# First sweep's rows 0 and 1 in 64-column halves, part of four norms on GpSimd, and constants and last stores on other queues

## The reference, cut to what matters

```python
# layer 0
u = par_u[0] * par_u[1] * (diag_u[:, None] * x[:2048] @ W_u) + x[:2048]     # the same for the other rows
e = concatenate([u, i])
h = adj @ (adj.T @ e)
x1 = layernorm(x + layernorm(h) * gamma + beta + x)
# layer 1, Chebyshev
T1 = adj @ x1
T2 = 2 * (adj @ T1) - x1
T3 = 2 * (adj @ T2) - T1
out = layernorm(x1 + x1 @ w[0] + T1 @ w[1] + T2 @ w[2] + T3 @ w[3] + bias)
```

## Time and profile before

| | us |
|---|---|
| median of 3 runs | 1199.03 |
| lowest and highest | 1196.73 and 1199.1 |
| profiled execution, its own time | 1196.89 |
| span of the profiled execution | 1195.1 |
| PE busy | 1105.3 (92%) |
| DVE busy | 920.1 (77%) |
| ACT, POOL busy | 334.6 (28%), 257.6 (22%) |

### The profile page before, as it was taken

The page is one execution under the profiler, slowest core; times in us unless marked ns, Lnnn a source line. Parts: engine busy times, 40 slices in busy tenths (PEclk is TensorE's granted clock), DMA queues, the critical chain, the costliest instruction groups (busy, mean ns, idle before and its releaser), DMA issues.

```text
span 1195.1 us, 13907 instructions
## 1 busy us (share of the span) xinstructions
PE 1105.3 (92%) x5004; PEld 479.5 (40%) x5004; DVE 920.1 (77%) x960; ACT 334.6 (28%) x598; POOL 257.6 (22%) x420
## 2 busy tenths in 40 slices
PE   4999999999999998799889999999899999988884
PEld 3444444444445453444333333444334444422221
DVE  2698798999899899698777766655577777678783
ACT  1456546546556555400101000000110000011111
POOL 0476645555354354100000000000000000001121
PEclk9999999999999999999999999999999999989998
DMA  7999999999999995899999999999599999999980
GB/s 225 305 286 297 295 281 314 280 300 301 284 296 271 289 286 131 193 300 306 237 346 346 338 318 314 296 295 255 145 334 347 336 341 348 307 315 346 343 235 11
DMA packets 362170, 340.33 MB, mean 285 GB/s; under 512 B 11292, under 2 KB 360772, under 8 KB 362132
## 3 DMA queue, kind: packets, MB, share of 16 engines
q1 hardware_dynamic: 253812, 232.11, 69.6%
q10 hardware_dynamic: 105600, 104.87, 30.3%
q0 software_dynamic: 2720, 2.86, 1.0%
HBM read 338.48 MB, written 1.31 MB: 284 GB/s over the span
## 4 chain that ended last, share of the span: by engine, by line
PE 57%; SPq 12%; DVE 12%; ACT 10%; issue 4%; ACTq 2%; POOL 1%; DMA 1%; DVEq 0%; POOLq 0%
PE bank L1219 30%; ACT terms L803 9%; SPq L372 7%; SPq L361 5%; DVE turned L531 4%; PE bank L1232 4%; PE bank L1287 4%; PE bank L1089 2%; PE bank L1049 2%; PE bank L1077 2%; ACTq L314 2%; PE bank L1101 2%; PE bank L1061 2%; DVE shared L551 2%; PE bank L1265 1%
## 5 line engine op out<-in xcount | busy, mean ns | idle before, releaser
L1219 PE MATMUL bank<-turned,terms 128*128 128x512 f32 x664 | 294.9, 597 | 4.5 <-DVE turned L531 3.2
L421 POOL COPY raw<-raw 32x512 f32<-32x512 f32 x320 | 194.7, 609 | 243.5 <-DVE raw L568 205.7
L551 DVE STREAM_TRANSPOSE shared<-shared 32x512 f32<-32x512 f32 x320 | 224.0, 700 | 4.1
L1049 PE MATMUL bank<-shared 128*64 128x256 f32 x1600 | 206.6, 385 | 6.3 <-DMA shared<-in_adj 6.2
L531 DVE STREAM_TRANSPOSE turned<-shared 128x2048 f32<-128x2048 f32 x70 | 160.4, 2302 | 59.9 <-PE bank L1219 37.0
L531 DVE STREAM_TRANSPOSE turned<-raw 128x2048 f32<-128x2048 f32 x70 | 159.8, 2297 | 53.4 <-PE bank L1219 38.4
L803 ACT COPY terms<-terms 32x512 f32<-32x512 f32 x320 | 197.1, 616 | 5.1 <-DVE terms L561 0.9
L1219 PEld LDWEIGHTS bank<-turned,terms 128*128 128x128 f32 x664 | 123.5, 190 | 165.6 <-issue 159.2
L466 POOL DMA_DIRECT2D out<-scratch x40 | 21.7, 549 | 667.3 <-DVE scratch L759 667.2
L1049 PEld LDWEIGHTS bank<-shared 128*64 128x64 f32 x1600 | 112.4, 136 | 87.6 <-issue 33.6
L794 ACT COPY scratch<-bank 128x512 f32<-128x512 f32 x80 | 46.6, 585 | 131.1 <-PE bank L1061 130.8
(11 more groups left out here) (150 smaller groups left out, 1048.1 us busy)
## 6 DMA issues: line engine op xcount, KB each, us to landing
shared<-in_adj SPq DMA_DIRECT2D x100, 1024.0 KB, 10.8
raw<-in_adj SPq DMA_DIRECT2D x100, 512.0 KB, 10.5
raw<-in_adj ACTq DMA_DIRECT2D x100, 512.0 KB, 12.3
shared<-in_adj SPq DMA_DIRECT2D x100, 512.0 KB, 10.2
shared<-in_adj ACTq DMA_DIRECT2D x100, 512.0 KB, 12.1
raw<-in_adj SPq DMA_DIRECT2D x80, 256.0 KB, 7.7
xq<-in_x POOLq DMA_DIRECT2D x40, 32.0 KB, 6.1
out<-scratch POOLq DMA_DIRECT2D x40, 32.0 KB, 4.6
```

Of the source, the lines that this page charges most:

```text
L421: last = nc.gpsimd.tensor_copy(moved[Q32 * c:Q32 * (c + 1), :, :, Q32 * q:Q32 * (q + 1)], beside[Q32 * q:Q32 * (q + 1), :, c, :, :])
L551: last = nc.vector.transpose(low_turned[Q32 * c:Q32 * (c + 1), :, :, Q32 * q:Q32 * (q + 1)], low[Q32 * q:Q32 * (q + 1), :, :, Q32 * c:Q32 ...
L1049: last = nc.tensor.matmul(t_bank[H * odd:H * (odd + 1), 0:PW], e[:, s * SB + b, :], panels[slot][:, s * SB + b, :], start=(k == 0 and b < ...
L1219: last = nc.tensor.matmul(sum_bank[parity][:, :], terms[:, c * GB + i, columns], turned[place][:, i * BANK:(i + 1) * BANK], start=(first a ...
```

## The change

Four things are changed.

1. The first sweep's rows 0 and 1: 16 of the 20 tiles go through `add_tile_p` with alternating halves, tiles 16 to 18 through the same function with all calls into one half (`together`), tile 19 as before. Each row has an odd bank of its own, which ScalarE copies out and `first_fold` adds back.
2. Step 2 of the norms 1 to 4 (add `xq`, square) runs on GpSimd.
3. ACT's queue issues `w_pair` and `par`; SP's queue issues `x` in five pieces, one semaphore each. The turn of `diag` waits for `diag_rows` alone.
4. Output rows: `turn_output` multiplies by `both` (two 64 x 64 identities stacked), which adds the two halves on TensorE, so that `finish` has one instruction less. Row 8 is stored by SP, row 9 half by SP and half by ACT.

```diff
@@ gpsimd
             nc.gpsimd.memset(terms[:, :, H:3 * H], 0.0).then_inc(zeroed, 1)
+            nc.gpsimd.memset(scratch[0:H, 2:4, :], 0.0).then_inc(zeroed, 1)
+            for n in range(1, NS):
+                y, sq = by_chunk(norm_terms[n], H), by_chunk(squares[:, :], H)
+                k = slice(2 * SEGS[n] * GB, 2 * (SEGS[n] + 1) * GB)
+                pool.wait_ge(norm_scaled, n)
+                nc.gpsimd.tensor_tensor(out=y, in0=y, in1=xq[:, k, :], op=ALU.add).then_inc(pool_step, 1)
+                pool.wait_ge(pool_step, 5 + n)
+                nc.gpsimd.tensor_tensor(out=sq, in0=y, in1=y, op=ALU.mult).then_inc(norm_squared, 1)
@@ vector, start
-            dve.wait_ge(consts_loaded, DMA * 8)
+            dve.wait_ge(diag_turned, 1)
+            chain(nc.vector.tensor_copy(diag[:, :], t_bank[:, 0:NB]))
+            dve.wait_ge(consts_loaded, DMA * 6)
...
-            dve.wait_ge(x_loaded, DMA)
-            for s in SEGS:
+            for k, s in enumerate(SEGS):
                 b = slice(s * SB, (s + 1) * SB)
+                dve.wait_ge(x_loaded[k], DMA)
@@ vector, norm_step
+                elif step == 2:
+                    pass
                 elif step == 3:
+                    if n >= 1:
+                        dve.wait_ge(norm_squared, n)
                     variance(sq, 2 * GB)
@@ vector, finish
-                halves = by_chunk(out_bank[n % 2][:, :], PH)
-                chain(nc.vector.tensor_copy(y, halves[:, :, 0:H]))
-                nc.vector.tensor_tensor(y, halves[:, :, H:PH], y, ALU.add).then_inc(out_taken, 1)
+                nc.vector.tensor_copy(y, by_chunk(out_bank[n % 2][:, 0:GB * H], H)).then_inc(out_taken, 1)
@@ tensor
-            def add_tile_p(t, place, c, parity, first, middle=None, diag=None):
+            def add_tile_p(t, place, c, parity, first, middle=None, diag=None, odd_sums=odd_bank, together=False):
...
-                    apart = i % 2 and diag is None
+                    apart = i % 2 and diag is None and not together
...
+            def first_fold(g):
+
+                pe.wait_ge(first_odd_copied, g + 1)
+                pe.wait_ge(zeroed, 3)
+                nc.tensor.matmul(sum_bank[g][0:H, :], both[:, :], scratch[:, 2 + g, :], start=False, stop=False,
+                                 skip_group_check=True)
+
             pe.wait_ge(zeroed, 2)
...
-                middle = {0: lambda: turn_h(NS - 1, SEGS[-1]), PAIR - 2: lambda: turn_q(0),
-                          PAIR - 1: lambda: turn_u(0)}.get(n)
-                add_tile(T1 + n, place1(g, c, n), c, g, n in (0, 2), n in (PAIR - 3, PAIR - 1), slice(0, PH), middle)
+                middle = {0: lambda: turn_h(NS - 1, SEGS[-1]), PAIR - 3: lambda: first_fold(0),
+                          PAIR - 2: lambda: (first_fold(1), turn_q(0)), PAIR - 1: lambda: turn_u(0)}.get(n)
+                if n == PAIR - 1:
+                    add_tile(T1 + n, place1(g, c, n), c, g, False, True, slice(0, PH), middle)
+                else:
+                    add_tile_p(T1 + n, place1(g, c, n), c, g, n in (0, 2), middle, None, first_odd_bank[g],
+                               n >= PAIR - 4)
...
-                    last = nc.tensor.transpose(out_bank[i % 2][:, c * P:(c + 1) * P], o_turned[:, c * P:(c + 1) * P],
-                                               ident[:, :])
+                    last = nc.tensor.matmul(out_bank[i % 2][:, c * H:(c + 1) * H], o_turned[:, c * P:(c + 1) * P],
+                                            both[:, :], start=True, stop=True)
```

71 lines of the change are left out of this document (49 added, 22 removed).

## The result

The changed kernel takes 1177.59 us (median of 4 runs, 1174.49 to 1178.97), the kernel before beside it 1198.23 us: a ratio of 0.9824, 95% interval 0.9806 to 0.9842, or 20.6 us less. A second measurement, further down, gave 1174.65 us and 0.9819 (0.9796 to 0.9842). The forecast was 1186.6 us with a range from 1182.5: the change is worth nearly twice what was forecast.

What follows compares the result with a forecast made beforehand. DMAs were taken to bound the kernel to about 166 us, then the loop; TensorE, by little, rows 0 and 1. Start 5.5 + rows 5.8 + end 0 = 11.3 us less, between 1185.6 and 1187.7: 1186.6 us, range 1182.5 to 1193.

Steps and rivals of the forecast that it cites:

- The rest after the last issue is taken as equal: End: after the last store's issue no time changes; the stores gain only 1.3 us of issue time.
- All of it is kept: Start: the whole 5.5 us gain lasts, as transfers to 166 us move as a block and the loop has room.
- Full rate then begins at about 9.5: Start: DMAs reach full rate where x ends, no longer at 15, so 5.5 us earlier.
- The rule quoted in the prediction: Start: a Trainium skill rule that spreading DMAs over queues saves only issuing time, usually small, as all share 16 engines.
- rival (a): Start: only issue time is saved, 3.1 us, giving 1189.0 us; chance 0.15.
- Forecast 5.8: First sweep, rows 0 and 1: gain 7.5 us, less 1.7 for folds, with VectorE the bound instead of TensorE.
- The gain of 1.0 ahead of turn 3: Rows 0 and 1: step 2 of norm 1, ahead of tile 3, gives 1.4 us less a wait for GpSimd.
- 1.7 charged for the folds: Rows 0 and 1: two folds of two MATMULs each give back 4 x 0.43 = 1.7 us.
- Rival (b): Rows 0 to 3: the sweep's loads don't follow, the 5.8 us are lost, 1192.4 us; chance 0.12.
- (c): Rival, rows 0 and 1: TensorE's clock falls to half; 1194.1 us, chance 0.05, or slower beyond that, chance 0.03.
- 0 forecast: Output rows: TensorE pays 0.6 us more a row, VectorE 0.44 less; 0 in rows 0 to 6.
- (d): Rival, output rows: they cost their 0.6 us everywhere and nothing comes back, +3.5 us, 1190.1 us; chance 0.07.

Runs made afterwards that it cites:

- t1_stores: The kernel before with only the stores of output rows 8 and 9 moved from GpSimd to SP and ACT: 1189.6 us, ratio 0.9932.
- t2_row9: The kernel before with only row 9's stores moved to SP and ACT, row 8 staying on GpSimd: 1190.29 us, ratio 0.9937.
- s_start: The kernel before with the changed start alone, constants on ACT and x in five pieces: 1194.71 us, ratio 0.9981.
- after_again: The changed kernel, unchanged, measured a second time: 1174.65 us, ratio 0.9819.
- a_old_output: The changed kernel with an output row's two halves added on VectorE after a transposition, as before: 1180.41 us, ratio 0.9842.

## Why the prediction was wrong

**The end: the step "The rest after the last issue is taken as equal" failed.** It gave the stores 1.3 us of issue time; they are worth 8.0 (t1_stores). What the runs show in its place is a DRAIN of 7.01 us on GpSimd's queue behind its last landed store. It grows with the number of DMAs that GpSimd issued (4.07 us for 49, 7.01 for 85), and it was off the path as soon as the last of these DMAs was issued 10.3 us ahead of the end (t2_row9). The trace before held the numbers: the last store lands at 1187.55, the DRAIN lasts from 1187.81 to 1194.82, and the span ends at 1195.1. I compared the issues and never read what lay between the last one and the span's end. Why the DRAIN takes longer behind more DMAs no record shows. The Trainium skill, Runtime: NRT & Kernel Launch, section "The ~15µs preamble/postamble breakdown", lists closing steps of 1.5, 1.5 and 2 us, in sum an estimate of 5 us, and says that the total depends on the engine count and the DMA setup. It names none that grows with the number of DMAs issued, as this DRAIN does in these traces.

**The start: the lead at panel 0 was there, "All of it is kept" failed.** The first panel piece was forecast near 8 and came at 6.01, and panel 0 moved by 6.1 us, in s_start and after_again by 6.7, where 5.5 was forecast. The step "Full rate then begins at about 9.5" was too good as well: from 10 to 15 us the rate was 310 GB/s in the changed kernel's first trace and 362 in its second, and panel 0's last piece landed 2.8 and 3.8 us earlier, not 5.5. So the 6 us at panel 0 are the arithmetic's lead: its scalars were there at 9.20 instead of 15.38. Panel 6 moved by 2.2 us (mean of the nine kernels with this start and all small loads where they were, 168.9, against 171.1 for the four with the old one), and the whole by 2.3 (s_start). I took panels 1 to 6 as one block of transfers that shifts by 5.5. The runs without the small loads show part of what it was instead: TensorE's own pace of 22.1 us a panel with GpSimd's small loads in the way, which cost 3.4 us by panel 6 with the old start (171.1 against 167.67) and 5.9 with the new one (168.9 against 163.00). Another 2.0 of the lead go ahead of panel 2 by something that no run isolates. The rule quoted in the prediction, by which only issue time is saved (3.1 us, rival (a)), met the result better than I did: the landing of panel 0 fits it, the copy of panel 0 doesn't.

**Rows 0 and 1: mechanism right, term too small.** Forecast 5.8; measured 6.8 from one profile of each kernel, 7.7 against the mean of the five with the old stage and all small loads. From 505 to 545 us VectorE waited 0.3 us once, turns lay some 3.0 apart, loads kept the pace at 307 GB/s, and GpSimd's wait cost 0.44 once, where 0.4 was forecast. From turn 3 to turn 16 the forecast had 44.9 us before and 38.4 after; the traces have 44.2 and 36.7, a gain of 7.5 instead of 6.5. I used 0.96 and 0.89 us for a variance and a scaling, which take 0.76 and 0.81 once VectorE doesn't wait for TensorE. The other two terms were off in opposite ways. The gain of 1.0 ahead of turn 3 isn't seen: the turn starts 49.9 and 49.7 us behind panel 19, against 49.2 before and up to 52.3 in other runs with the old stage. And of the 1.7 charged for the folds hardly anything shows: from turn 16 to row 0's end it is 10.4 us instead of 10.2, and from there to row 1's 11.4 instead of 11.5. Rival (b) is refuted. Of (c), the clock stayed at 1.00 from 505 to 545 us.

**Output rows: right, as far as the runs can tell.** 0 forecast, none found by a_old_output within its interval of some 3 us either way. (d), which would be 3.5, is not borne out; a cost of about 1 us would not be seen.

**The sum.** 8.0 + 2.3 + 6.8 to 7.7 are 17.1 to 18.0 of the 20.6. The single profiles differ by 1.7 more between the sweeps and 2.8 in the outputs, and both go with the granted clock (0.88 and 1.00, 0.95 and 0.97), at either value in kernels whose code there is the same. That the change didn't cause this remainder is argued from the table, not shown by an experiment.

The range failed for a reason of form as well. The good ends of all terms that I had listed add up to 17.0 us, 1180.9 from where the forecast starts; I put the lower end at 1182.5, and both lie above the 1177.6 measured. A place that I took as equal without reading it had no term at all.

## What to carry to other kernels

Read the last microseconds of the span as a stage of their own: if the last DMAs are GpSimd's, the time behind their landing is a term, and moving the last few stores to another queue takes it away. Read the sequencers' instructions there too, since the timeline leaves them out. A lead won at the start is worth what is left of it at the first milestone that another resource sets, so follow it through each repeat of the loop rather than once. When two engines are within a few per cent of each other, as TensorE and VectorE are in rows 0 and 1, relieving one is worth little and relieving both more than the sum: here 2.9 and 0.3 us alone, 7.5 together, from turn 3 to turn 16.
